# A recommender's forward pass in sixteen tiles: four table look-ups per tile one tile ahead instead of three two tiles ahead, with a rearranged setup

## What is computed

```python
emb = embed_table[f_ix, x_idx]                       # (2048, 26, 16)
lin1 = w1_table[f_ix, x_idx].sum(axis=1, keepdims=True) + w1_bias
s = emb.sum(axis=1)
fm = 0.5 * ((s * s).sum(-1) - (emb * emb).sum(axis=(1, 2)))[:, None]
h = relu(emb.reshape(n, 416) @ mlp_w1 + mlp_b1)
h = relu(h @ mlp_w2 + mlp_b2)                        # 400 wide
mlp_out = h @ mlp_w3 + mlp_b3
x0 = emb.transpose(0, 2, 1); last = x0
for W in (cin_w0, cin_w1, cin_w2):                   # (128, 26, 26), (128, 128, 26) x 2
    last = jnp.einsum('ndl,ndf,klf->ndk', last, x0, W); feats.append(last)
cin_result = concatenate(feats, -1).sum(axis=1) @ lin_w + lin_b
return lin1 + fm + mlp_out + cin_result
```

## Time and profile before

| | |
|---|---|
| median of 3 runs | 530.3 us (530.12 to 530.62) |
| the profiled execution's own time | 530.45 us |
| its span, first to last instruction | 528.6 us, mean granted TensorE clock 0.968 |
| PE, DVE, ACT, POOL busy | 89%, 71%, 68%, 69% of the span |

### The profile page before, as it was taken

One profiled execution on the slowest core, in us unless ns is written; L12 is line 12 of the kernel. 1 busy time (PEld: TensorE's weight loads), 2 busy tenths in 40 slices (PEclk: granted clock), 3 DMA queues, 4 the chain that ended last, 5 costly groups with the idle time before them and its releaser, 6 DMA issues. The chain is left out here.

```text
span 528.6 us, 6627 instructions
## 1 busy us (share of the span) xinstructions
PE 468.6 (89%) x2230; PEld 384.6 (73%) x2230; DVE 376.7 (71%) x610; ACT 361.6 (68%) x707; POOL 364.6 (69%) x382
## 2 busy tenths in 40 slices
PE   0798499899898989899999989898989899998895
PEld 0795367588787878687877878787868687787684
DVE  6811265869687786868686968778686868695766
ACT  1002459878686877777676868786777767677883
POOL 5777787877777777777777777777777777774000
PEclk9999559899999999999999999999999999999998
DMA  8973652122222222222222222222222222221000
...
DMA packets 21550, 13.63 MB, mean 26 GB/s; under 512 B 12792, under 2 KB 20493, under 8 KB 21261
## 3 DMA queue, kind: packets, MB, share of 16 engines
...
## 5 line engine op out<-in xcount | busy, mean ns | idle before, releaser
L417 POOL DMA_INDIRECT emb<-rows,idx_raw x377 | 364.3, 966 | 117.4 <-issue 114.6
L660 DVE TENSOR_TENSOR z_lo<-ps_s,z_hi 128x512 fp32r<-128x512 f32 (+1 forms) x192 | 130.7, 687 | 66.5 <-ACT ps_s L483 65.1
L476 ACT ACTIVATE z_hi<-ps_s 128x512 fp32r<-128x512 f32 (+1 forms) x192 | 114.4, 596 | 78.7 <-PE ps_s L908 77.8
L483 ACT ACTIVATE ps_s<-ps_s 128x512 f32<-128x512 f32 (+1 forms) x192 | 113.9, 593 | 0.7
L922 PE MATMUL ps_q<-z_lo,zw_hi 128*127 128x512 f32 (+1 forms) x192 | 86.0, 448 | 15.9 <-DVE z_lo L660 14.4
L923 PE MATMUL ps_q<-z_hi,zw_lo 128*127 128x512 f32 (+1 forms) x192 | 76.4, 398 | 0.0
L924 PE MATMUL ps_q<-z_hi,zw_hi 128*127 128x512 f32 (+1 forms) x192 | 76.3, 397 | 0.0
L908 PE MATMUL ps_s<-xt,pick 128*128 128x512 f32 (+1 forms) x192 | 74.3, 402 | 0.4 <-DVE xt L652 0.4
L922 PEld LDWEIGHTS ps_q<-z_lo,zw_hi 128*127 128x127 f32 (+1 forms) x192 | 36.4, 190 | 32.4 <-DVE z_lo L660 19.7
L994 PE MATMUL ps_y<-look_hi,one_hot 128*128 128x442 f32 (+1 forms) x156 | 56.3, 361 | 2.3 <-DVE one_hot L754 2.3
L995 PE MATMUL ps_y<-look_lo,one_hot 128*128 128x442 f32 (+1 forms) x156 | 54.8, 353 | 0.0
...
## 6 DMA issues: line engine op xcount, KB each, us to landing
emb<-rows,idx_raw POOLq DMA_INDIRECT x377, 3.0
...
w<-cin_w SPq DMA_DIRECT2D x1, 832.0 KB, 6.7
w<-cin_w ACTq DMA_DIRECT2D x1, 832.0 KB, 13.2
w_space<-cin_w SPq DMA_DIRECT2D x1, 832.0 KB, 15.0
w_space<-cin_w ACTq DMA_DIRECT2D x1, 832.0 KB, 18.4
...
```

The source lines that it names most:

```text
L417: pool.indirect_dma_start(emb[t % EMB][:, f, :], None, rows, bass.IndirectOffsetOnAxis(row_ix[:, t, f:f + 1], 0)).then_inc(gathered[t], 16)
L476: act.activation(z_hi[0:k, c, :], ps[0:k, :], ACT.Square)
L483: act.activation(ps[0:k, :], ps[0:k, :], ACT.Square).then_inc(hi_ready, 1)
L660: dve.tensor_tensor(z_lo[0:k, u % NC, :], ps_s[s_no(t, u) % RING][0:k, :], z_hi[0:k, u % NC, :].bitcast(F32), ALU.subtract).then_inc(lo_re ...
```

## The change

**Look-ups.** `LOOKS` is 4 (the four last fields), `FIRST_LOOK` 2, `LEAD` 1: during tile t the four look-ups of tile t + 1 are made, for t = 1 to 14, so there are 56 in place of 39, and 360 gathers in place of 377. Their rows stand behind the chunks 2, 4, 6 and 8, and DVE picks them at its chunks 5, 7, 9 and 11. The keys of all tiles are transposed once in the setup, stored to DRAM, and loaded per tile as `key_row`, spread over all partitions, by SP; the `keys` matmuls are gone. A row matmul now waits for the pick before it.

**A tile.** The transposes `x_half` stand behind the chunks 10 and 11 instead of 9 and 10, and ACT squares chunk 11 ahead of `copy_by_position`. The copy into `x32` leaves `x_high` and becomes `x_full`, behind `square(t, 0)`; `picked` of chunks 1 and 2 waits for it. `hidden2` has 10 matmuls instead of 12; ACT and DVE have a small operation more each around it.

**The last tile.** The transposes of tile 15 stand behind `hidden2` and `sum_products` of tile 14, and its `by_pos` is copied in three pieces, of which the last waits for the last 4 gathers alone.

**Setup.** `cin_w2` is loaded in two halves of 64 layers each (two DMAs per issuing engine), `cin_w1` is issued when the first half has landed, and the 26 matmuls are made per half, 52 in all. The rearrangement through DRAM takes 6 stores and 6 loads instead of 3 stores and 53 loads (besides those of `yl`, which stay). `mlp_w2` is loaded and split during tile 0, where a fourth table is also split. Some buffers share their room.

```diff
-LOOKS = 3
-FIRST_LOOK = 3
-LEAD = 2
+LOOKS = 4
+FIRST_LOOK = 2
+LEAD = 1
+EARLY = 18
...
-        LOOK_SPLIT = {4: 0, 6: 1, 8: 2}
-        KEYS = {1: 0, 5: 1, 9: 2}
-        ROWS = {3: 0, 7: 1, 11: 2}
-        PICKED = {5: 0, 9: 1}
-
-        CONSTS = 15
-        MOVES = [N1 + N1 + N1 + 2, N2 + N2 + 2, N3 + 2]
+        LOOK_SPLIT = {3: 0, 5: 1, 7: 2, 9: 3}
+        KEYS = {3: 0, 5: 1, 7: 2, 9: 3}
+        ROWS = {2: 0, 4: 1, 6: 2, 8: 3}
+        PICKED = {5: 0, 7: 1, 9: 2, 11: 3}
...
+        def leave(eng, n):
+
+            name, g, c0, col, ab, n_b, n_c, n_d = BLOCKS[n]
+            n_a, here = GROUPS[g], {"y12": y12, "y13": y13, "y23": y23}[name]
+            run = n_c * n_d
+            order = [[run, n_a], [n_a * run, n_b]] if ab else [[run, n_b * n_a]]
+            eng.dma_start(bass.AP(y_dram[n].tensor, y_dram[n].offset, order + [[1, run]]),
+                          here[:, c0:c0 + run]).then_inc(y_stored[n], 16)
+
+        def move(eng, n):
+
+            name, g, c0, col, ab, n_b, n_c, n_d = BLOCKS[n]
+            n_a = GROUPS[g]
+            eng.wait_ge(y_stored[n], 16)
+            eng.dma_start(moved[0:n_a * n_c, g, col:col + n_b * n_d].rearrange("p (b d) -> p b d", d=n_d),
+                          bass.AP(y_dram[n].tensor, y_dram[n].offset,
+                                  [[n_d, n_a * n_c], [n_a * n_c * n_d, n_b], [1, n_d]])).then_inc(moved_in[g], 16)
...
-            sp.wait_ge(idx0_in, 16)
-            sp.dma_start(w2[0:HALF_P], cin_w2[0:HALF_P]).then_inc(w2_in, 16)
+            for h in range(2):
+                ls = slice(HALF_P * h, HALF_P * (h + 1))
+                sp.dma_start(w2[0:HALF_P, ls], cin_w2[0:HALF_P, ls]).then_inc(w2_in[h], 16)
+            sp.wait_ge(w2_in[0], 16 * 2)
             sp.dma_start(w1[0:HALF_P], cin_w1[0:HALF_P]).then_inc(w1_in, 16)
...
-            for n, (dram, here) in enumerate(((y12_dram, y12), (y13_dram, y13), (y23_dram, y23), (yl_dram, yl))):
-                sp.wait_ge(y_copied, n + 1)
-                sp.dma_start(dram, here[:]).then_inc(y_stored[n], 16)
+
+            for n, copies in enumerate((1, 1, 1, 2, 2, 3)):
+                sp.wait_ge(y_copied, copies)
+                leave(sp, n)
+            sp.wait_ge(y_copied, 4)
+            sp.dma_start(yl_dram, yl).then_inc(y_stored[6], 16)
+            sp.wait_ge(keys_copied, 1)
+            sp.dma_start(key_dram, key_t[:]).then_inc(keys_stored, 16)
             sp.wait_ge(moved_zeroed, 1)
-            sp.wait_ge(y_stored[0], 16)
-            W = NX_
-            move(sp, 0, WO[1], N2, N2, N1, y12_dram, 0, N2 * W, N2, W)
-            move(sp, 0, XO + X12 + X13, N2, N3, N1, y12_dram, X12, N2 * W, N3, W)
-            sp.wait_ge(y_stored[3], 16)
+            for n in range(3):
+                move(sp, n)
+            sp.wait_ge(y_stored[6], 16)
             move_lin(sp, 0, F2, N2, 0, 0, N2)
             move_lin(sp, 0, F3, N3, 0, X12, N3)
-            move(sp, 1, XO + X12, N1, N3, N2, y12_dram, X12 + X13, W, N3, N2 * W)
...
+                    sp.wait_ge(m2_zeroed, 1)
+                    sp.dma_start(m2_raw[:, 0:3, :], mlp_w2[0:3 * P, :].rearrange("(c k) h -> k c h", k=P)).then_inc(m2_in, 16)
+                    for r in (0, 32, LO):
+                        sp.dma_start(m2_raw[r:r + HR, 3, :], mlp_w2[3 * P:H, :]).then_inc(m2_in, 16)
+                    for r in (32, LO):
+                        sp.dma_start(m2_raw[r + HR:r + HR + 1, 3, :], mlp_b2.rearrange("(o h) -> o h", o=1)).then_inc(m2_in, 16)
...
+            for t in range(FIRST_LOOK, T):
+                if t >= FIRST_LOOK + 2:
+                    sp.wait_ge(one_hot_ready, look_no(t - 2, LOOKS))
+                sp.dma_start(key_row[t % 2], key_dram[LOOKS * t:LOOKS * (t + 1), :].partition_broadcast(P)
+                             ).then_inc(keys_in[t % 2], 16)
...
+            def copy_last_early():
+                act.wait_ge(gathered[T - 1], 16 * EARLY)
+                act.wait_ge(looked, look_no(T - 1, LOOKS))
+                for fs in (slice(0, EARLY), slice(F - LOOKS, F)):
+                    act.activation(by_pos[:, :, fs], emb[(T - 1) % EMB][:, fs, 0:D].rearrange("p f d -> p d f"), ACT.Copy)
+
+            def copy_last_late():
+                fs = slice(EARLY, F - LOOKS)
+                act.wait_ge(gathered_late, 16 * (F - LOOKS - EARLY))
+                act.activation(by_pos[:, :, fs], emb[(T - 1) % EMB][:, fs, 0:D].rearrange("p f d -> p d f"),
+                               ACT.Copy).then_inc(by_pos_ready, 2)
...
-                act.activation(x32[t % 2][LO * h:LO * h + XR], ps, ACT.Copy)
                 act.activation(xt[t % 2][0:XR, 4 * h:4 * h + 4, :], ps, ACT.Copy).then_inc(hi_ready, 1)
+
+            def x_full(t, h):
+                act.wait_ge(lo_ready, x_no(t, h) + 1)
+                act.activation(x32[t % 2][LO * h:LO * h + XR],
+                               ps_s[x_no(t, h) % RING][0:XR, :].rearrange("p (c n) -> p c n", c=4),
+                               ACT.Copy).then_inc(x32_ready, 1)
...
-                    if u == NU - 1 and t + 1 < T:
+                    square(t, u)
+                    if u == NU - 1 and t + 1 < T - 1:
                         copy_by_position(t + 1)
-                    square(t, u)
+                    if u == NU - 1 and t + 1 == T - 1:
+                        copy_last_early()
+                        copy_last_late()
                     if t == 0 and u in LOOK_SPLIT:
                         look_high(LOOK_SPLIT[u])
+                    if t == 0 and u == 8:
...
-                for u in range(NC):
-                    square(t, u)
+                square(t, 0)
+                x_full(t, 0)
+                x_full(t, 1)
+                square(t, 1)
+                square(t, 2)
...
+                    if t == 0 and u == 10:
+                        second_low()
                     if looks(t + LEAD):
                         if u in PICKED:
                             pick_row(t + LEAD, PICKED[u])
-                        if u - 2 in KEYS:
-                            keys_to_one_hot(t + LEAD, KEYS[u - 2])
+                        if u in KEYS:
+                            keys_to_one_hot(t + LEAD, KEYS[u])
+
...
+            def start_last():
+                t = T - 1
+                times_left(t - 1, NQ - 1)
+                times_third(t - 1)
+                add_third(t - 1)
+                add_product(t - 1, NQ - 1)
+                fold(t - 1)
+                hidden2(t - 1)
+                x_low(t, 0)
+                x_low(t, 1)
+                for u in range(NC):
+                    z_low(t, u)
...
-                dve.wait_ge(keys_out, look_no(t, i) + 1)
-                dve.tensor_tensor(one_hot[:], ps_y[:, 0:P].unsqueeze(1).to_broadcast([P, SHARES, P]),
+                if i == 0:
+                    dve.wait_ge(keys_in[t % 2], 16 * ((t - FIRST_LOOK) // 2 + 1))
+                if look_no(t, i):
+                    dve.wait_ge(rows_out, look_no(t, i))
+                dve.tensor_tensor(one_hot[:], key_row[t % 2][:, i:i + 1, :].to_broadcast([P, SHARES, P]),
                                   share_row.unsqueeze(2).to_broadcast([P, SHARES, P]),
...
-            pe.wait_ge(w2_in, 16 * 2)
             pe.wait_ge(lin_in, 16 * 3)
-            for g in range(F):
-                mm = pe.matmul(ps_y[:, g:g + 1], w2[:, :, g], lin[:, 2:3], start=True, stop=True)
+            for h in range(2):
+                ls = slice(HALF_P * h, HALF_P * (h + 1))
+                pe.wait_ge(w2_in[h], 16 * 2)
+                for g in range(F):
+                    mm = pe.matmul(ps_y[ls, g:g + 1], w2[:, ls, g], lin[:, 2:3], start=True, stop=True)
             mm.then_inc(m_done, 1)
...
+            pe.transpose(ps_s[0][0:T * LOOKS, 0:P], look_key[:].rearrange("p t i -> p (t i)"), ident).then_inc(keys_out, 1)
...
+                if u in (1, 2):
+                    pe.wait_ge(x32_ready, 2 * t + u)
...
+                for c in range(3):
+                    pe.matmul(ps_mlp[:, 0:H], h1t_lo[:, c, :], m2_hi[:, c, :], start=(c == 0), stop=False)
+                    pe.matmul(ps_mlp[:, 0:H], h1t_hi[:, c, :], m2_lo[:, c, :], start=False, stop=False)
+                    pe.matmul(ps_mlp[:, 0:H], h1t_hi[:, c, :], m2_hi[:, c, :], start=False, stop=False)
+                mm = pe.matmul(ps_mlp[:, 0:H], h1t_rest[:], m2_rest[:], start=False, stop=True)
...
-            def keys(t, i):
-
-                n = look_no(t, i)
-                if n == 0:
-                    pe.wait_ge(look_step, 10)
-                if n:
-                    pe.wait_ge(looked, n)
-                pe.matmul(ps_y[:, 0:P], look_key[:, t, i:i + 1].to_broadcast([P, P]), ident,
-                          start=True, stop=True).then_inc(keys_out, 1)
...
-                    if u == 1 and t:
+                    if u == 1 and 0 < t < T - 1:
                         sum_products(t - 1)
                     if u == 2:
                         hidden1(t)
...
                     if u == 8 and after is None:
```

(44 more changed lines are left out.)

160 lines of the change are left out of this document (92 added, 68 removed).

## The result

The changed kernel takes 576.35 us (median of 4 runs, 574.51 to 577.56) where the kernel before takes 530.21 on the same chip: ratio 1.0866, interval 1.0836 to 1.0896. The forecast was 566 (542 to 580), slower with 0.88. The profiled execution has a span of 575.7 us.

What follows compares the result with a forecast made beforehand. PE's stream and its waits within each tile were taken as the bound. From 528.6 us: +42.6 tiles 1 to 14, +3.8 tile 0, -5.5 first matmuls, -4.5 DRAM trip, -0.5 last tile gave 564.5, plus 1.85: 566 us (542 to 580).

Steps and rivals of the forecast that it cites:

- Setup, first matmuls: `cin_w2` matmuls in the setup start at about 9.5 and end at 22.5 us: -5.5 us (-6.6 to +5.3).
- DRAM trip: Setup rearrangement through DRAM: fewer transfers spare issue time, not the two round trips: -4.5 us (0 to -8).
- Tile 0: ACT, busiest there, also splits a fourth table and `mlp_w2`: +3.8 us (0 to 6).
- Tiles 1 to 13: Each of these tiles takes 31.1 us against 28.5 before (30.3 to 31.9 if the walk is believed).
- The walk: Step-by-step timing of one tile across PE, ACT and DVE, zero at look-up 0's row matmuls' end: PE waits 4.25 us.
- Tile 14: Tile whose transposes come behind `hidden2`, fold and `sum_products`: 3 us later than the others, 34.0 us in all.
- Last tile: The end of the kernel, tile 15, gets shorter: -0.5 us.
- The row matmuls did not fill PE's waits: Rival: row matmuls fill PE's waits, shrinking them to 1 us per tile, 27.2 us tiles, 512 us; chance 0.11.
- The milder loss: Rival: DVE makes picks 1 to 1.5 us earlier, tiles of 29.5 to 30 us, 544 to 551 us; chance 0.07.
- The clock didn't fall in each tile: Rival: PE's clock falls in each tile, 3 us of work at half clock, +42, 608 us; chance 0.04.
- the gathers bound the end: Rival: 360 gathers at 1.27 us set a 501 us floor, binding at 26.5 us tiles or less; within the 0.11.
- POOL idle before L470: Sign in the changed profile: at 31.1 us per tile POOL waits for free buffers instead of bounding the end.

Runs made afterwards that it cites:

- experiment 3: Changed kernel with the earlier three look-ups two tiles ahead, transposes and plain last tile, keeping the new setup: 531.26 us, ratio 1.0025 to the kernel before.
- experiment 4: experiment 3 with full copies ahead of `square(0)`, `sum_products` behind `hidden1`, `z_low(2)` ahead of `hidden2`, fold and pick: 526.06 us, 0.9921 of the kernel before.
- experiment 1: Changed kernel with only `LEAD` 2 and `FIRST_LOOK` 3, look-ups made two tiles ahead: 553.79 us, ratio 1.0426 to the kernel before.
- experiment 2: Changed kernel with DVE's last pick ahead of `z_low(11)` and the add, and the last tile treated like the others: 557.11 us, 1.0493 to the kernel before.

## Why the prediction was right, and what it missed

**Setup, first matmuls: -5.5 forecast, -5.9 measured.** They start at 10.56 (forecast 9.5), the 104 last 11.54, the first product is at 36.15 instead of 42.06. I had chosen 13 between 11.9 and 23.8; the row lies below both ends. It bears out what the Trainium skill (TensorE: Matmul & The Clock Gate, section LDWEIGHTS) says: a weight load costs by its columns. Here 104 loads of 64 columns took 11.54 us, where 52 of 128 had taken 11.91, both at a granted clock of 1.00. That -5.9 is so near to -5.5 is in part luck: the start came 1.1 later and the matmuls 1.5 shorter than forecast, and the two cancel.

**DRAM trip: -4.5 forecast, -2.5 measured.** From the first product to the end of the group matmuls (61.78) are 25.6 us, 28.1 before. The step that failed is "all three sums should come close together at about +13.5". Close together they are, but at +15.3 and +16.4: DVE waits 13.77 for the scratch instead of 15.03, so fewer transfers took only 1.3 off the wait for the first sum. The other half of the gain, 1.2, is that the group matmuls now run without a wait, in 9.6 us instead of 10.9. Together `main(0, 0)` starts 8.4 earlier, not 10. Kernels with the same setup had `main(0, 0)` at 67.1 to 70.4 (68.43 in experiment 3), so a single start is good to some 2 us.

**Tile 0: +3.8 forecast, +4.2 measured.** Right by size; the cause that I gave is not shown. ACT does have 1.58 us more for a fourth table and 1.72 for `mlp_w2`. But experiment 3 splits no fourth table, and its tile 0 lasts 34.0 us where that of the changed kernel lasts 33.5; that of experiment 4, without it too, lasts 32.05. What the split alone costs stays open.

**Tiles 1 to 13: 31.1 forecast, 31.5 measured.** The walk can be laid beside the rows. A gap is the distance between two starts less the slots between (0.233 for 512 columns, 0.18 for the 400 of `hidden2`, 0.35 for four transposes): ahead of the transposes 285.87 - 284.30 - 0.23 = 1.34.

| PE stands ahead of | forecast | measured |
|---|---|---|
| transposes, for the copy | 1.2 | 1.34 |
| `picked(0)` | 0.5 | 0.61 |
| `picked(1)`, `picked(2)`, `main(0)` | 1.1 | 0.59 + 0.47 |
| `main(1)` | 0.25 | 0.44 |
| `main(2)` | 0.15 | 0 |
| rows 2 | 0.75 | 0.84 |
| rows 3 | 0.3 | 0.40 |
| sum | 4.25 | 4.69 |

Work and the slower matmul behind each wait make the other 26.8, as forecast (31.1 - 4.25 = 26.85). Every wait stood where the walk had put it but that for `z_lo` at L1048, which PE met one instruction earlier as the wait for the full copy (L540). I had placed this "within that gap"; both indeed end together, and the price is the same. Experiments 1 and 2 show that the largest of these waits is a cost by itself: taken away in two ways, wholly (1.34) and down to 0.27, it gave 1.35 and 1.09 per tile, and nothing of it came back. The other gaps were only argued, from the same rows.

**Tile 14: 34.0 forecast, 36.4 measured.** In the walk's time, whose zero is 521.17 here, the transposes came at 20.8 (forecast 20.3), `picked(0)` at 23.3 (22.4), `main(15, 0)` at 27.5 (25.2). Two things were missing: with DVE done, the full copies, which I had hidden behind DVE's operations, stand alone ahead of `picked(1)` (2.25 us); and PE's clock fell. Experiment 2 shows that the whole excess of 6.0 over a tile and 0.5 of the next belong to the special end, in a tile that makes look-ups; what it costs behind a tile without them, as in experiment 1, no run tells.

**Last tile: -0.5 forecast, +0.5 measured.** The forecast gave no working for its 0.5. From `main(15, 0)` on, 7 slots ran at the low clock, at 0.43 instead of 0.233: 1.4.

**The sum: 564.5 forecast, 575.7 measured.** Of the 11.2 us, tiles 1 to 13 are 5.7, tile 14 2.4, the setup 1.6, the last tile 1.0, tile 0 0.4. Nearly all terms erred to the same side: 35.9 us more than before were forecast, 47.1 were measured.

**Rivals.** The row matmuls did not fill PE's waits, since these are at other places. The milder loss is half borne out by experiment 2: the pick came 1.1 earlier and the tile 1.1 shorter, but at 30.4 us that is above the 29.5 to 30 of the rival, and of the way to 557 us a third is the plain end. The clock didn't fall in each tile: by the windows of the changed kernel the granted clock is 1.00 from 130 to 530 us. That the gathers bound the end was never near at 31.5 us, and is true in experiment 4.

**A sign that was wrong:** POOL idle before L470. It has 112.2 us of idle, 109.4 of it the 0.3 us between two gathers, as when it never rests. With 22 gathers, 27.9 us per tile, it gains 3.6 per tile but begins far behind (52 gathers for two tiles), and to its last gather, issued at 464.35, it never had to wait for a free buffer, as the prediction said it would. Nothing hung on it.
